# Context copies on ScalarE, router weights turned by TensorE, and additions in halves: one change to a two-layer attention kernel

## Chip, core and metric

The kernel runs on one core of a Trainium2 chip. The metric is the device time of one execution in microseconds (us); lower is better. The engines are TensorE (PE, its weight loads are PEld), VectorE (DVE), ScalarE (ACT), GpSimd (POOL) and SyncE (SP, which only issues DMAs here). Each runs its own list of instructions in the order in which it was written, and they meet through semaphores.

## What is computed

Two transformer layers with adaptive layer norm (six modulation rows from a condition vector), on 4 batches of 1024 tokens of width 128. Cut to what matters:

```python
# layer 0, attention: 16 heads of 64, causal
q, k, v = split(einsum('bse,ehd->bshd', x, w_qkv))
probs = softmax(where(mask, q @ k.T / sqrt(64), neg));  out = (probs @ v) @ w_out
# layer 0, second half: mixture of depths. 127 of the 1024 tokens are routed
weights = (x @ router_w)[..., 0] + router_b[0]
topv, topi = top_k(weights, 128);  sel = weights > topv[:, -1]
sel_idx = sort(topi[:, :127]);  x_sel = x[sel_idx]
hn = rmsnorm(x_sel, ln1)        # small attention (rope, masked), then
x2 = x1 + gelu(rmsnorm(x1, ln2) @ w1) @ w2      # x1 = x_sel + attention
out = scatter(x2 * weights[sel_idx]) + x * (1 - sel)
# layer 1: attention with 16 heads of 8 and a 3D rope, then 8 experts, best 2 of them
# a gate of layer 0 or 1 is sign(g) * max(|g|, 0.25), with sign(0) = 1
```

## The kernel before

**First attention (layer 0).** Heads go in pairs; there are 8 pairs for each batch, 32 in all (`n`, in batch `a = n // 8`). A pair has 12 items `m`: two halves `c` of 512 queries, and in each the key tiles `j` up to the diagonal. For an item TensorE makes transposed scores (`st_item`) in one pair of banks, ScalarE takes their exponentials (`exp_item`, L1524), TensorE multiplies them by the values (`pv_item`) and adds up in bank 4, and GpSimd adds the exponentials for the softmax sums (`add_up`, L816: `p_sum += ring`, 10 additions for each pair). The first tile of a half (`m` = 0 and `m` = 4) is written into `p_sum` itself, the others into a ring of three. Meanwhile the row maxima of pair `n + 1` are made: TensorE `max_item`, VectorE `row_max` (L1943). When a half is complete its contexts leave bank 4 for `oT` (`contexts`, L1964, VectorE, 128x512), and the first `pv_item` of the next half waits for that copy (semaphore `o_out`).

**Second attention (layer 1).** Its steps (`step1`) are others: VectorE takes maxima of 128x1024 (L2342), ScalarE exponentials of 128x512 (L1765). Twenty-three steps of its lead lie in the last pair of a first attention.

**The side chain.** All the rest (norms, modulation, routing, the routed tokens' attention and FFN, layer 1's projections, experts) is a serial chain of named steps, `MOD0`, `ADD1`, `MOD_ATTN`, `PREP`, `LNA`, `MOE`. `slots_of` spreads the chain of batch `a` over the 96 items of that batch's pairs, at equal distances; each engine does its part of a step at the end of its part of that item, ScalarE one item later. Names with `~` have no work on TensorE. The others use one bank (bank 5, `side`), in order: `side_free` makes TensorE wait until the step before has been read out (`side_out`). For the last batch the chain runs between the steps of the second attention (`late_steps_of`).

The places that matter here:

- `mod0` and `mod1` (L1539, L1545): TensorE makes modulation rows in `side`, ScalarE copies them out, VectorE's `gates` (L1926) makes five passes over two rows in SBUF (sizes 128x256).
- `w0`, `w1`, `~wcol`: the router weights come out as a row repeated on all partitions, `w_row`; VectorE needs them as columns `w_col`, one per tile of 128 tokens. It multiplies each tile by the identity and sums along the row (L2083, 8 instructions of 128x128), then copies to `extra` (L2085, L2086).
- `rmsnorm` (L2141 to L2144), in `pickT0` and `wo0`: a chain of 9 instructions for the inverse root on 128x1, in `rsqrt` (L1886): `scalar_tensor_tensor` and `tensor_tensor`, each waiting for the one before. The layer norms use the same `rsqrt` on 128x8.
- `row_max` of an item stands in VectorE's list behind whatever side step came before it, and TensorE's `max_item` waits until the maxima two uses earlier have left the bank.

What GpSimd does for an item, as it was:

```python
sv = p_sum[(2 * n + c) % 3][:, :, lo:]
pool.tensor_tensor(sv, sv, ring0[SLOT[m]][:, :, 0:HALF - lo], ALU.add).then_inc(sem("added"), 1)
```

## Time and profile before

| | us |
|---|---|
| median of 3 runs | 2725.14 (2724.52 to 2730.5) |
| the profiled execution | 2733.0 |
| its span, first to last instruction | 2731.2 |
| busy in it: TensorE | 2183.8 (80%) |
| VectorE | 1627.4 (60%) |
| ScalarE | 1276.4 (47%) |
| GpSimd | 804.2 (29%) |
| first attention's 8 pairs of batch 0 | 58 to 390 |
| batch 1, with side chain | 390 to about 745 |
| second attention of batch 0 | to 973 |
| first attention, batch 2 / batch 3 | 973 to 1384 / 1637 to 2047 |
| second attention, batch 1 / 2 / 3 | to 1637 / 2368 / 2652 |
| remaining chain of the last batch | 2652 to 2731 |

The engines work at the same time, so their busy times don't add up to the span. An engine's idle time matters only where another engine's wait follows from it. The profile names for each idle stretch what ended it. The granted clock is the share of TensorE's full 2.4 GHz; it stands at 1.0 or 0.5 at any moment, and a stretch shows the mean.

### The profile page before, as it was taken

What the parts mean: (1) busy time and instruction counts of PE and PEld (TensorE: products, weight loads), DVE (VectorE), ACT (ScalarE), POOL (GpSimd) and SP (SyncE); (2) the same over time, 40 slices, a digit from 0 to 9 for tenths busy, and PEclk for the clock granted to TensorE, in tenths of its full rate; (3) what the DMA queues carried; (4) which work ended last, traced back from release to release, by engine and by line L of the source; (5) the groups of instructions that cost most, each with busy time, mean ns of one, the idle gap of its engine ahead of it and who ended that gap; (6) DMA issues with size and microseconds to landing.
All of it is one profiled execution on the core that took longest, in us unless ns stands there. A gap on an engine that the chain in (4) does not pass through costs nothing.

```text
span 2731.2 us, 39653 instructions
## 1 busy us (share of the span) xinstructions
PE 2183.8 (80%) x14753; PEld 896.9 (33%) x14757; DVE 1627.4 (60%) x2829; ACT 1276.4 (47%) x2289; POOL 804.2 (29%) x618
## 2 busy tenths in 40 slices
PE   3989998899777887889868778888877677667876
PEld 2434443444321133444312123344432222121112
DVE  3454446556678556555676745655576776487732
ACT  1433333343358743343347763233336466537873
POOL 0665563443500033443411103443343000001203
PEclk9999998999899998989989998898998898869999
DMA  3000001001110010000210000000021100110000
GB/s 79 15 23 15 20 23 35 23 27 35 35 42 14 1 30 12 15 19 27 66 40 20 12 4 27 19 15 27 12 65 38 47 1 16 59 34 3 5 3 8
DMA packets 81199, 69.14 MB, mean 25 GB/s; under 512 B 46672, under 2 KB 62800, under 8 KB 80496
## 3 DMA queue, kind: packets, MB, share of 16 engines
q1 hardware_dynamic: 81008, 66.60, 9.0%
q8 instruction: 119, 1.95, 0.3%
q14 instruction: 72, 0.59, 0.1%
HBM read 57.58 MB, written 8.98 MB: 24 GB/s over the span
## 4 chain that ended last, share of the span: by engine, by line
PE 61%; DVE 22%; ACT 9%; issue 6%; SPq 2%; DMA 1%; POOL 0%; ACTq 0%; POOLq 0%; DVEq 0%
PE banks L875 59%; DVE pmax L2342 5%; ACT ring L1765 3%; DVE part_max L1943 2%; ACT p_sum L1765 1%; ACT room L1572 1%; SPq L666 1%; DVE ntmp L1892 1%; PE banks L1014 1%; DVE ntmp L1847 1%; DVE pick L2083 1%; DVE rstd L1894 1%; DVE h L1911 1%; DVE room L2092 1%; DVE stats L1899 1%
## 5 line engine op out<-in xcount | busy, mean ns | idle before, releaser
L816 POOL TENSOR_TENSOR p_sum<-p_sum,ring 128x1024 f32<-128x1024 f32 (+3 forms) x320 | 548.9, 1715 | 810.5 <-PE banks L875 453.0
L2342 DVE TENSOR_REDUCE pmax<-banks 128x2 f32<-128x1024 f32 x512 | 610.5, 1222 | 187.9 <-PE banks L875 184.6
L1943 DVE TENSOR_REDUCE part_max<-banks 128x2 f32<-128x1024 f32 (+3 forms) x384 | 365.8, 958 | 336.7 <-PE banks L875 334.2
L875 PE MATMUL banks<-ring,v 128*9 128x512 f32 (+4 forms) x2816 | 565.5, 581 | 0.0
L875 PE MATMUL banks<-qT,kT 64*128 64x512 f32 (+4 forms) x2048 | 468.3, 521 | 100.1 <-DVE pmax L2342 52.4
L1765 ACT ACTIVATE ring<-banks 128x512 f32<-128x512 f32 x768 | 416.3, 596 | 144.7 <-PE banks L875 141.5
L1524 ACT ACTIVATE ring<-banks 128x1024 f32<-128x1024 f32 (+3 forms) x320 | 245.7, 768 | 473.9 <-PE banks L875 468.6
L875 PE MATMUL banks<-oT 64*128 64x512 bf16 x1024 | 185.2, 397 | 91.6 <-ACT ring L1765 41.7
L875 PEld LDWEIGHTS banks<-qT,kT 64*128 64x128 f32 (+1 forms) x2048 | 147.7, 169 | 325.0 <-issue 101.5
L875 PE MATMUL banks<-p_sum,v 128*9 128x512 f32 (+1 forms) x768 | 220.4, 644 | 31.9 <-DVE oT L1964 26.3
L847 POOL TENSOR_TENSOR room<-room 128x512 f32<-128x512 f32 x32 | 40.6, 1270 | 691.5 <-ACT room L1572 691.5
L875 PE MATMUL banks<-k_bf,q_bf 64*128 64x512 bf16 (+3 forms) x768 | 133.8, 342 | 92.6 <-DVE part_max L1943 91.9
L1765 ACT ACTIVATE p_sum<-banks 128x512 f32<-128x512 f32 x256 | 139.0, 595 | 75.7 <-PE banks L875 75.7
L875 PEld LDWEIGHTS banks<-ring,v 128*9 128x9 f32 (+1 forms) x2816 | 95.2, 112 | 151.2 <-issue 76.4
L875 PE MATMUL banks<-kT,qT 64*128 64x512 bf16 x512 | 105.4, 408 | 45.5 <-ACT ring L1765 29.5
L875 PEld LDWEIGHTS banks<-oT 64*128 64x128 bf16 x1024 | 42.5, 94 | 299.4 <-ACT ring L1765 164.5
L794 POOL CAST q_bf<-qT 128x512 bf16<-128x512 f32 x64 | 39.3, 614 | 317.8 <-ACT qT L1482 317.7
L875 PE MATMUL banks<-hT,w_qk 128*128 128x512 f32 x256 | 129.9, 632 | 1.5 <-ACT hT L1529 0.9
L875 PE MATMUL banks<-m_row,ones_bf 64*128 64x512 bf16 (+3 forms) x768 | 130.7, 333 | 0.0
L1524 ACT ACTIVATE p_sum<-banks 128x1024 f32<-128x1024 f32 x64 | 65.5, 1023 | 123.3 <-PE banks L875 123.2
L1938 DVE COPY kT<-banks 128x512 f32<-128x512 f32 x64 | 43.3, 689 | 107.7 <-PE banks L875 107.1
L822 POOL TENSOR_TENSOR oT<-oT,inv_bc 128x1024 f32<-128x1024 f32 x32 | 76.3, 2385 | 90.9 <-DMA inv_bc<-softmax_inverses 90.9
(270 smaller groups left out, 2624.7 us busy)
## 6 DMA issues: line engine op xcount, KB each, us to landing
inv_bc<-softmax_inverses SPq DMA_DIRECT2D x64, 256.0 KB, 4.0
w_qk<-in_L_attn_w_qkv SPq DMA_DIRECT2D x64, 64.0 KB, 2.1
low<-in_L_ffn_attention_mask SPq DMA_DIRECT2D x4, 1024.0 KB, 6.1
stage<-rope_constants SPq DMA_DIRECT2D x4, 1024.0 KB, 4.8
x_b<-in_L_attn_x SPq DMA_DIRECT2D x4, 512.0 KB, 4.6
w_v<-in_L_attn_w_qkv SPq DMA_DIRECT2D x32, 64.0 KB, 2.1
stage<-in_L_ffn_w SPq DMA_DIRECT2D x8, 256.0 KB, 6.2
out<-x_b SPq DMA_DIRECT2D x16, 128.0 KB, 1.8
```

The source lines that it names most:

```text
L666: sp.dma_start(dst[rows, :, :], src[par, :, 2 * g:2 * g + 2, :]).then_inc(sem(f"stacks{g}"), 16)
L794: pool.tensor_copy(q_bf[:, cols], qT[q][:, cols]).then_inc(sem("qb_cast"), 1)
L816: pool.tensor_tensor(sv, sv, ring0[SLOT[m]][:, :, 0:HALF - lo], ALU.add).then_inc(sem("added"), 1)
L822: pool.tensor_tensor(ov, ov, inv_bc[:, :], ALU.mult).then_inc(sem("o_norm"), 1)
L847: pool.tensor_tensor(pv[:, 0:4, :], pv[:, 0:4, :], pv[:, 4:8, :], ALU.add).then_inc(sem("halved"), 1)
L875: return pe.matmul(dst, lhsT, rhs, start=start, stop=stop)
L1014: last = pe.transpose(side[:, (t % 4) * P:(t % 4 + 1) * P], src[:, t, :], eye)
L1524: act.activation(dst, banks[1][:, :, lo:HALF], ACT.Exp, scale=SCALE0).then_inc(sem("expd"), 1)
L1765: act.activation(ring1[n % 8], bank[ST1_BANK[n % 3]][:, :], ACT.Exp, scale=SCALE).then_inc(sem("expd1"), 1)
L1938: dve.tensor_copy(kT[n % 2][:, c * HALF:(c + 1) * HALF], bank[6 + c][:, :]).then_inc(sem("k_evac"), 1)
L1943: dve.reduce_max(part_max[:, :, t, c], banks[MAX_PAIR[m]][:, :, 0:w], AX).then_inc(sem("row_max"), 1)
L2342: dve.reduce_max(pmax1[:, :, g, t, c], banks[(0, 3)[USE1[b]["max", m] % 2]][:, :, :], AX).then_inc(sem("row_max1"), 1)
```

## The change

- `contexts` goes from VectorE's list to ScalarE's. There it stands behind the exponentials of the first item of the next half: half 0 of a pair behind `exp_item(n, 4)`, half 1 behind `exp_item(n + 1, 0)`. In the last pair of batches 1 to 3 half 1 stands behind its own last item.
- `add_up` makes two additions in place of one, one for each head of the pair, the second waiting for the first (new semaphore `added0`).
- `~wcol` becomes `wcol`, with work on TensorE: eight transposes of a 1x128 piece of `w_row` into one column each of `side`; VectorE copies the eight columns twice out of the bank. The row numbers in `extra` are written once, at setup.
- `mod0` and `mod1` have no copy on ScalarE; VectorE reads the bank itself, and `gates` has three instructions, of which the first two read the bank. The step `~gates0` is gone, and so the other steps of each chain lie up to one item earlier.
- `rmsnorm` uses a new `rsqrt_column`: nine `tensor_scalar` instructions whose second operand is a column of scalars. The layer norms keep `rsqrt`.

```diff
...
-MOD0 = ["mod0", "~gates0"]
+MOD0 = ["mod0"]
 ADD1 = ["mod1", "ctxT0", "ctxT1", "wo1_0", "wo1_1"]
...
        + [f"ex{n}" for n in range(2 * T)] + ["~moe"])
-MOD_ATTN = ["~lnb_a", "~lnb_b", "lnb0", "lnb1", "w0", "w1", "~wcol", "~larger0", "~larger1", "nb", "~sel", "thr", "slots", "~pick", "gather", "idx",
+MOD_ATTN = ["~lnb_a", "~lnb_b", "lnb0", "lnb1", "w0", "w1", "wcol", "~larger0", "~larger1", "nb", "~sel", "thr", "slots", "~pick", "gather", "idx",
             "pickT0", "pickT1", "maskrows", "hn1", "trig", "qkv", "rot0", "msel", "~kdiag", "sc0", "sc1", "pT0", "sc2", "pT1", "sc3", "pT2", "pT3",
...
                     sv = p_sum[(2 * n + c) % 3][:, :, lo:]
-                    pool.tensor_tensor(sv, sv, ring0[SLOT[m]][:, :, 0:HALF - lo], ALU.add).then_inc(sem("added"), 1)
+                    pool.tensor_tensor(sv[:, 0, :], sv[:, 0, :], ring0[SLOT[m]][:, 0, 0:HALF - lo], ALU.add).then_inc(sem("added0"), 1)
+                    pool.wait_ge(sem("added0"), NA * n + ADDED[m])
+                    pool.tensor_tensor(sv[:, 1, :], sv[:, 1, :], ring0[SLOT[m]][:, 1, 0:HALF - lo], ALU.add).then_inc(sem("added"), 1)
...
                 yield "mod0"
-                yield "~gates0"
...
                     yield f"w{c}"
-                for s in ("~wcol", "~larger0", "~larger1"):
-                    yield s
+                side_free(("wcol", b))
+                read_out(pe, ("w1", b))
+                for t in range(T):
+                    last = pe.transpose(side[:, t:t + 1], w_row[0:1, t * P:(t + 1) * P], eye[0:1, 0:1])
+                last.then_inc(sem("side_mm"), 1)
+                yield "wcol"
+                yield "~larger0"
+                yield "~larger1"
                 side_free(("nb", b))
...
             def mod0_side(b):
-                filled(act, ("mod0", b))
-                copy(mod0[b % 2][:, :, :].rearrange("p a d -> p (a d)"), side[:, :]).then_inc(sem("side_out"), 1)
                 yield "mod0"
-                yield "~gates0"
             def add1_side(m):
-                if m:
-                    act.wait_ge(sem("x_final"), T // 2 * m)
-                filled(act, ("mod1", m))
-                copy(mod1[:, :, :].rearrange("p a d -> p (a d)"), side[:, 0:2 * D]).then_inc(sem("side_out"), 1)
                 yield "mod1"
...
                     yield f"w{c}"
-                for s in MOD_ATTN[MOD_ATTN.index("~wcol"):MOD_ATTN.index("pickT0")]:
+                for s in MOD_ATTN[MOD_ATTN.index("wcol"):MOD_ATTN.index("pickT0")]:
                     yield s
...
+            def contexts(n, c):
+                act.wait_ge(sem("pv"), NI * n + (4 if c == 0 else NI))
+                if n >= OSLOTS:
+                    a, p = divmod(n - OSLOTS, NP)
+                    if p < OUT_PAIRS:
+                        filled(act, ("op0_1", a))
+                    elif a == 0:
+                        filled(act, ("op1_1", a))
+                    else:
+                        act.wait_ge(sem("out_mm"), 2 * a)
+                copy(oT[n % OSLOTS][:, c * HALF:(c + 1) * HALF], bank[4][:, :]).then_inc(sem("o_out"), 1)
...
                     exp_item(n, m)
+                    if m == 4:
+                        contexts(n, 0)
+                    if m == 0 and (p or a == 1):
+                        contexts(n - 1, 1)
+                    if m == NI - 1 and p == NP - 1 and a:
+                        contexts(n, 1)
                     if m == ROWS1_AT + 1:
...
             link(dve.tensor_scalar(an, an, 3.1415925, -3.1415925, ALU.min, ALU.max))
+            link(dve.tensor_copy(extra[:, :, 1], const("row")))
             dve.memset(extra[:, :, 0:1], 0.0).then_inc(sem("setup_dve"), 1)
...
                     link(dve.scalar_tensor_tensor(dst, t_, 1.5, cur, ALU.add, ALU.mult))
+                    cur = dst
+            def rsqrt_column(dst, src, bits, t_):
+                link(dve.tensor_scalar(bits, src.bitcast(I32), 1, None, ALU.logical_shift_right))
+                link(dve.tensor_scalar(bits, bits, -1.0, RSQRT_MAGIC, ALU.mult, ALU.add))
+                cur = bits.bitcast(F32)
+                for _ in range(3):
+                    link(dve.tensor_scalar(t_, cur, cur, -0.5, ALU.mult, ALU.mult))
+                    link(dve.tensor_scalar(t_, t_, src, 1.5, ALU.mult, ALU.add))
+                    link(dve.tensor_scalar(dst, t_, cur, None, ALU.mult))
                     cur = dst
...
-            def gates(mod, g):
+            def gates(dst, g):
                 ga = tmp[:, 0:2 * D].rearrange("p (a d) -> p a d", a=2)
-                link(dve.scalar_tensor_tensor(ga, g, -1.0, g, ALU.mult, ALU.max))
-                link(dve.tensor_scalar(ga, ga, 0.25, None, ALU.max))
-                link(dve.tensor_scalar(g, g, 0.0, 2.0, ALU.is_ge, ALU.mult))
-                link(dve.tensor_scalar(g, g, -1.0, None, ALU.add))
-                link(tt(g, g, ga, ALU.mult))
+                link(dve.tensor_scalar(dst, g, 0.0, 0.5, ALU.is_ge, ALU.subtract))
+                link(dve.scalar_tensor_tensor(ga, dst, 4.0, g, ALU.mult, ALU.mult))
+                return dve.scalar_tensor_tensor(dst, ga, 0.5, dst, ALU.max, ALU.mult)
...
-            def contexts(n, c):
-                dve.wait_ge(sem("pv"), NI * n + (4 if c == 0 else NI))
-                if n >= OSLOTS:
-                    a, p = divmod(n - OSLOTS, NP)
-                    if p < OUT_PAIRS:
-                        filled(dve, ("op0_1", a))
-                    elif a == 0:
-                        filled(dve, ("op1_1", a))
-                    else:
-                        dve.wait_ge(sem("out_mm"), 2 * a)
-                dve.tensor_copy(oT[n % OSLOTS][:, c * HALF:(c + 1) * HALF], bank[4][:, :]).then_inc(sem("o_out"), 1)
...
                 filled(dve, step)
-                dve.wait_ge(sem("gates0"), a + 1)
+                read_out(dve, ("mod0", a))
                 residual(xs3[a % 3], c, side[:, :], mod0[a % 2][:, 0, :]).then_inc(sem("side_out"), 1)
...
             def mod0_side(b):
+                m = mod0[b % 2]
+                filled(dve, ("mod0", b))
+                new = side[:, :].rearrange("p (a d) -> p a d", a=4)
+                link(dve.tensor_copy(m[:, 1, :], new[:, 1, :]))
+                link(dve.tensor_scalar(m[:, 2, :], new[:, 2, :], 1.0, None, ALU.add))
+                gates(m[:, 0::3, :], new[:, 0::3, :]).then_inc(sem("side_out"), 1)
+                read_out(dve, ("mod0", b))
                 yield "mod0"
-                read_out(dve, ("mod0", b))
-                m = mod0[b % 2]
-                gates(m, m[:, 0::3, :])
-                dve.tensor_scalar(m[:, 2, :], m[:, 2, :], 1.0, None, ALU.add).then_inc(sem("gates0"), 1)
-                yield "~gates0"
...
                 x = xs3[m % 3]
+                if m:
+                    dve.wait_ge(sem("x_final"), T // 2 * m)
+                filled(dve, ("mod1", m))
+                gates(mod1[:, :, :], side[:, 0:2 * D].rearrange("p (a d) -> p a d", a=2)).then_inc(sem("side_out"), 1)
+                read_out(dve, ("mod1", m))
                 yield "mod1"
-                read_out(dve, ("mod1", m))
-                gates(mod1, mod1[:, :, :])
                 yield "ctxT0"
...
                 filled(dve, ("lnb1", b))
-                dve.wait_ge(sem("gates0"), b + 1)
+                read_out(dve, ("mod0", b))
                 dve.wait_ge(sem("ln_b_h"), T * (b + 1))
...
                 yield "w1"
-                read_out(dve, ("w1", b))
-                for t in range(T):
-                    dve.scalar_tensor_tensor(ties[:, t, :], w_row[:, t * P:(t + 1) * P], 1.0, eye, ALU.mult, ALU.mult, accum_out=w_col[:, t:t + 1]).then_inc(sem("w_col"), 1)
-                dve.wait_ge(sem("w_col"), T * (b + 1))
-                link(dve.tensor_copy(extra[:, :, 0], w_col[:, :]))
-                link(dve.tensor_copy(extra[:, :, 1], const("row")))
-                yield "~wcol"
+                filled(dve, ("wcol", b))
+                link(dve.tensor_copy(extra[:, :, 0], side[:, 0:T]))
+                dve.tensor_copy(w_col[:, :], side[:, 0:T]).then_inc(sem("side_out"), 1)
+                read_out(dve, ("wcol", b))
+                yield "wcol"
                 if b:
...
                     link(dve.tensor_scalar(nvar[:, 0:1], nvar[:, 0:1], RMS_EPS, None, ALU.add))
-                    rsqrt(rstd[:, 0:1], nvar[:, 0:1], nbits[:, 0:1], ntmp[:, 0:1])
+                    rsqrt_column(rstd[:, 0:1], nvar[:, 0:1], nbits[:, 0:1], ntmp[:, 0:1])
                     dve.scalar_tensor_tensor(hn[:, :], src, rstd[:, 0:1], ln_rows[:, n, :], ALU.mult, ALU.mult).then_inc(sem("hn"), 1)
...
                                 final_max(n + 1, 0)
-                    if m == 4:
-                        contexts(n, 0)
                     if m == 5 and (p or a == 1):
                         invert(n - 1)
-                    if m == NI - 1:
-                        contexts(n, 1)
                     for step in SLOT_STEPS[a][p * NI + m]:
...
```

ScalarE's list in the second pair of batch 0, from `m` = 2 to `m` = 6, as it was (`p_sum` and `ring` are the exponentials, `m_row`, `qT` and `v` the next pair's row maxima, queries and values):

```order
L1524 ACTIVATE ring<-banks 128x2x128
L1482 ACTIVATE m_row<-banks 128x512
L1482 ACTIVATE qT<-banks 128x512 x2
L1524 ACTIVATE p_sum<-banks 128x1024
L1524 ACTIVATE ring<-banks 128x1024
L1482 ACTIVATE v<-banks 128x512 x2
```

and as it is now:

```order
L1531 ACTIVATE ring<-banks 128x2x128
L1489 ACTIVATE m_row<-banks 128x512
L1489 ACTIVATE qT<-banks 128x512 x2
L1531 ACTIVATE p_sum<-banks 128x1024
L1489 ACTIVATE oT<-banks 128x512
L1531 ACTIVATE ring<-banks 128x1024
L1489 ACTIVATE v<-banks 128x512 x2
```

The context copy stands between the exponentials of items 4 and 5. It stands in the same way behind the `p_sum` of item 0.

VectorE's list in batch 2's side chain, where the router weights become columns, as it was (`part_max` and `max_cols` are the row maxima of the next pair, `cnt` counts larger weights):

```order
L1938 COPY kT<-banks 128x512 x2
L1964 COPY oT<-banks 128x512
L1847 TENSOR_TENSOR h<-h,mod 128x8x128
L1943 TENSOR_REDUCE part_max<-banks 128x2 x2
L1970 RECIPROCAL inv_pk<-den_pk 128x16
L2083 SCALAR_TENSOR_TENSOR pick,w_col<-w_row,consts 128x128 x8
L2085 COPY h<-w_col 128x8
L2086 COPY h<-consts 128x8
L1943 TENSOR_REDUCE part_max<-banks 128x2
L2092 TENSOR_SCALAR room,cnt<-w_row,w_col 128x1024
```

and as it is now:

```order
L1967 COPY kT<-banks 128x512 x2
L2103 COPY h<-banks 128x8
L2104 COPY w_col<-banks 128x8
L1972 TENSOR_REDUCE part_max<-banks 128x2 x2
L1986 RECIPROCAL inv_pk<-den_pk 128x16
L2111 TENSOR_SCALAR room,cnt<-w_row,w_col 128x1024
```

The `oT` copy is gone from here, eight multiplications and two copies have become two copies, and the step stands one item earlier, ahead of the two maxima of item 5; the counting (`~larger0`) follows those maxima directly.

## Rows read from the trace of the kernel before

**Rows 1.** Stretches from:to in us, length, each engine's busy us; PEclk is the granted clock.

```profile
core 0: us, PE busy (x) PEld busy (x) DVE busy (x) ACT busy (x) POOL busy (x), PEclk, DMA share, GB/s
58.00:390.00 332.00, 310.37 (x2284) 138.94 (x2282) 154.95 (x216) 126.84 (x173) 188.75 (x132) 0.97 0.08 20
322.90:356.80 33.90, 32.94 (x254) 14.36 (x248) 14.63 (x19) 13.81 (x20) 21.61 (x16) 1.00 0.10 23
390.00:706.00 316.00, 277.02 (x1890) 140.58 (x1890) 190.41 (x395) 109.98 (x182) 131.82 (x91) 0.92 0.10 28
600.60:651.40 50.80, 48.09 (x348) 26.27 (x345) 31.36 (x70) 17.09 (x24) 21.66 (x15) 1.00 0.11 36
1009.00:1328.00 319.00, 270.28 (x1808) 134.33 (x1808) 187.68 (x350) 106.41 (x177) 127.02 (x88) 0.89 0.08 22
1671.00:1987.00 316.00, 268.07 (x1804) 133.06 (x1801) 187.17 (x350) 106.77 (x179) 126.69 (x88) 0.89 0.07 18
```

**Rows 2.** TensorE's waits, 58 to 390 us: total us, times, longest.

```profile
PE banks L875 <- DVE part_max L1943: 14.1, 11, 7.9
```

**Rows 3.** TensorE's waits, 390 to 706 us.

```profile
PE banks L875 <- DVE part_max L1943: 12.4, 7, 5.3
PE banks L875 <- DVE oT L1964: 10.6, 6, 2.8
...
PE banks L1176 <- DVE hn L2144: 3.5, 1, 3.5
```

**Rows 4.** TensorE's waits, 1009 to 1328 us.

```profile
PE banks L875 <- DVE part_max L1943: 30.4, 11, 6.9
...
PE banks L875 <- DVE oT L1964: 4.0, 4, 3.4
```

**Rows 5.** Timeline around `~wcol` of batch 2: start, us, instruction, [idle before it].

```profile
1051.55 2.36 POOL L816 TENSOR_TENSOR p_sum<-p_sum,ring 128x1024 f32<-128x1024 f32 x1 [0.28 <-ACT ring L1524]
...
1051.56 2.49 DVE L2083 SCALAR_TENSOR_TENSOR pick<-w_row,consts 128x128 f32<-128x128 f32 x1
...
1062.43 0.61 PE L875 MATMUL banks<-k_bf,q_bf 64*128 64x512 bf16 x2 [6.89 <-DVE part_max L1943]
```

**Rows 6.** Timeline at the second `rmsnorm` of batch 2's chain.

```profile
1210.26 2.35 DVE L1892 SCALAR_TENSOR_TENSOR ntmp<-nbits 128x1 f32<-128x1 f32 x1
...
1219.48 0.29 PE L875 MATMUL banks<-k_bf,q_bf 64*128 64x128 bf16 x2 [6.70 <-DVE part_max L1943]
```

**Rows 7.** Groups by line and shape, whole span: busy us, mean ns of one | idle before.

```profile
L816 POOL TENSOR_TENSOR p_sum<-p_sum,ring 128x1024 f32<-128x1024 f32 x128 | 301.1, 2352 | 319.2 <-PE banks L875 201.2 <-ACT ring L1524 118.0
...
L816 POOL TENSOR_TENSOR p_sum<-p_sum,ring 128x512 f32<-128x512 f32 x64 | 82.8, 1294 | 92.5 <-ACT ring L1524 89.6
...
L1014 PE MATMUL banks<-consts,h 128*128 128x128 f32 x128 | 27.6, 354 | 62.4 <-DVE h L1911 59.9 <-ACT den_rows L1482 1.5 <-ACT hT L1529 0.9
...
L849 POOL TENSOR_TENSOR room<-room 128x256 f32<-128x256 f32 x32 | 23.3, 728 | 2.5
...
L1892 DVE SCALAR_TENSOR_TENSOR ntmp<-rstd 128x1 f32<-128x1 f32 x16 | 11.4, 714 | 0.6
```

**Rows 8.** One line's instructions: ns min/median/max of one, first and last start.

```profile
L2142 DVE TENSOR_SCALAR nvar<-nvar x8: 153/154/154, 491.1 to 2291.5; 128x1 f32<-128x1 f32 x8
```

**Rows 9.** The same for the multiplications of `~wcol`.

```profile
L2083 DVE SCALAR_TENSOR_TENSOR pick<-w_row,consts x32: 279/289/2494, 436.1 to 2162.9; 128x128 f32<-128x128 f32 x32
```

**Rows 10.** Timeline where half 0's contexts leave bank 4, a pair of batch 0.

```profile
144.09 1.02 ACT L1524 ACTIVATE p_sum<-banks 128x1024 f32<-128x1024 f32 x1 [0.68 <-PE banks L875]
...
146.99 0.68 DVE L1964 COPY oT<-banks 128x512 f32<-128x512 f32 x1
...
147.81 1.08 PE L875 MATMUL banks<-p_sum,v 128*64 128x512 f32 x4 [0.20 <-DVE oT L1964]
```

**Rows 11.** Timeline: a pair's last two additions, and item 1's exponential of the next.

```profile
131.33 2.13 POOL L816 TENSOR_TENSOR p_sum<-p_sum,ring 128x512 f32<-128x512 f32 x2
...
135.23 0.81 ACT L1524 ACTIVATE ring<-banks 128x768 f32<-128x768 f32 x1 [1.28 <-PE banks L875]
```

More of the change, by code:

```diff
@@ L490, in adaln_kernel @@
                  den_stored den_loaded inv_den inv_stored inv_loaded o_norm out_mm res_a
-                 ln_a_h ln_b_h ln_c_h ln_d_h gates0 w_col larger thr_part sel trig_rep pick mask_pick hn rot_s k_diag mask_sel sc_max sc_exp proc
+                 ln_a_h ln_b_h ln_c_h ln_d_h larger thr_part sel trig_rep pick mask_pick hn rot_s k_diag mask_sel sc_max sc_exp proc
                  split_h split_m split_l rope1 rest1
                  s1_mm row_max1 nmax_hl mrow1_mm mrow1 st1_mm expd1 pv1 o1_raw ctx_raw ctx1
-                 lg_sub lg_exp coef halved moe gated x_final
+                 lg_sub lg_exp coef added0 halved moe gated x_final
         """.split() + [f"scratch_{a}{part}" for a in "qk" for part in "hml"] + [f"stacks{g}" for g in range(NG)] + [f"x_in{n}" for n in range(3)]
```

## The prediction

> **What bounds the kernel now.** I read the busy times by stretch first, because a share over the whole span mixes two kinds of stage. In the first attention of batch 0 TensorE is the bound: an undisturbed pair takes 33.90 us and TensorE is busy for 32.94 of them, at clock 1.00 [rows 1]. In the same attention of batches 1, 2 and 3 the side chain runs along. A pair can still go at full clock there (50.80 us with 48.09 busy, in the stretch where the chain has the most matmul work), but over the eight-pair stretches TensorE is idle for 39, 49 and 48 us, and the granted clock is 0.92, 0.89 and 0.89 [rows 1]. The last two batches have the same numbers within 3 us, so I work out batch 2 and count it twice.
>
> Next come the waits: who makes TensorE idle? Nearly always VectorE, and under two names. The row maxima (`part_max`) cost 14.1, 12.4 and 30.4 us in batches 0, 1 and 2, and the context copy (`oT`) 10.6 and 4.0 us in batches 1 and 2 [rows 2 to 4]. Neither is slow itself. Both stand in VectorE's list behind a side step. So the third view is the timeline just before a wait. At 1062.43 TensorE goes on after 6.89 us of idling for a maximum. Before that VectorE was in the multiplications of `~wcol`, one of which took 2.49 us, starting and ending with a GpSimd addition of 2.36 us [rows 5]. The same instruction has a minimum of 279 ns and a median of 289 [rows 9]. In `rmsnorm` an operation on 128x1 takes 2.35 us, and TensorE's wait at the end of that chain is 6.70 us [rows 6]; its mean over 16 is 714 ns [rows 7]. But the `tensor_scalar` on 128x1 in the same chain never took more than 154 ns, all eight of them [rows 8]. So some of VectorE's instructions wait until the running GpSimd addition is over, and others never do. That is what four of the change's five edits touch.
>
> **Edit 1, contexts on ScalarE.** VectorE loses 64 copies of 0.68 us, ScalarE gets 64. In an undisturbed pair TensorE waited 0.20 us for the copy [rows 10]. On ScalarE it starts when the exponential ends, 144.09 + 1.02 = 145.11, and even at VectorE's 0.68 us it is over by 145.8, two microseconds before TensorE's 147.81. So the wait goes: 8 x 0.2 = 1.6 us in batch 0. ScalarE is busy for a third to two fifths of these stretches, and what stands behind the copy on it, the next exponential, waits for TensorE. I take nothing as its cost. In batches 1 to 3 the waits of 10.6, 4.0 and again 4.0 us go, 18.6. In the last pair of these batches the copies lie among maxima of the second attention, with VectorE the engine that ends the waits; two copies of 0.68 in each of three give 4 us. Together **24 us**.
>
> **Edit 2, `wcol` on TensorE.** VectorE's part falls from eight multiplications and two copies to two small copies out of a bank. The longest waits, 5.3 in batch 1 and 6.9 in batch 2, lie on it [rows 3, 4]; I take them as gone: 5.3 + 6.9 + 6.9 = **19 us**. It adds eight transposes to TensorE. The trace has none of 1x128. The nearest are those of 128x128, 27.6 us for 128 [rows 7], or 0.22 each, so 1.7 us for eight at the most; the least is nothing. I take 1 us, four times: -4. In batch 3's chain, which lies in the second attention, no addition runs: there eight times 0.289 us become two copies, **2 us** at most.
>
> **Edit 3, `rmsnorm` on columns.** It has nine instructions as before. If a `tensor_scalar` with a column of scalars behaves like the one with a constant [rows 8], none waits for GpSimd. Batches 1 to 3 have two each. Waits that go with them: 3.5 in batch 1 and, of the other maxima waits there (12.4 - 5.3 = 7.1 in six), about 4; in batch 2 6.7 and one that I put at 5 of the remaining 30.4 - 6.9 - 6.7; batch 3 as batch 2. That is 7.5 + 11.7 + 11.7 = 31, less 1 us for each of the six that stays, since the first and last instruction of a `rmsnorm` still read two arrays of 128x128: **25 us**.
>
> **Edit 4, additions in halves.** GpSimd's additions take 2352 ns for 1024 columns and 1294 for 512, that is 236 ns fixed; the step from one to the next dependent one is 2.5/32 = 0.08 us [rows 7]. An addition becomes 0.31 us longer, and 320 of them 100 us. Is GpSimd's list on the path? The nearest place is the ring: a pair's last addition ends at 131.33 + 2.13 = 133.46, and the exponential that may need its slot starts at 135.23, 1.8 us later [rows 11]. Half 1 has seven additions, 2.2 us more in all, part of which goes into the idle time ahead of them (0.28 us ahead of the one in [rows 5]). So it just fits, at nothing. The gain: a VectorE instruction waits for the rest of 1.29 us, not of 2.35. On the layer norms' `rsqrt`, which is not changed, it takes perhaps 5 of batch 0's 14.1 us [rows 2], and 2 us in each other batch: **11 us**.
>
> The Trainium skill, "SBUF — State Buffer", section "Who interferes with whom", has this as an exclusive lock on a port pair that VectorE and GpSimd share, held for the whole instruction; by that rule the trace agrees (2.49 us beside 2.36). The same page counts `tensor_scalar` among those that can take the pair. By that, edit 3 would bring nothing, and the sum below would be 25 us smaller plus its share of clock; the 154 ns of a 128x1 speak against it.
>
> **Edit 5, gates from the bank.** Of five or six instructions on SBUF arrays two now remain that read no bank. In batches 2 and 3 the `mod0` step lies on a maxima wait; I take 2 us each: **4 us**. VectorE now waits for TensorE's matmul in the very item of the step, behind which the next maxima are queued: at `mod0` and `wcol`, some 0.5 us six times, -3. In the last chain, where nothing covers it, `ctxT0` comes after three VectorE operations and no longer after one copy: -1.
>
> **The clock.** Where the clock is low TensorE's work takes twice its time. The loss is the missing share times the busy time: 0.08 x 277 = 22, 0.11 x 270 = 30 and again 30, 82 us in all [rows 1]. The granted clock is 1.00 in the pairs with little idling and 0.89 to 0.92 where there is much [rows 1]. As some two thirds of the waits on VectorE go, but not all and not the ones for norms, I take half: **41 us**. Bounds are 0 and 82.
>
> **Sum:** 24 + 19 + 2 + 25 + 11 + 4 + 41 = 126, less 4 + 3 + 1 = 8, gives 118 us. The profiled execution has a span of 2731.2 us and took 2733.0; the runs' median is 2725.1. Off the span that gives 2613; off the median **2607 us**.
>
> **Rivals.**
>
> A. The waits pass to the next thing. All steps come up to an item earlier, and a side step of 2 us, ahead of a maximum, makes TensorE wait even with no GpSimd in play. Then half of the 83 us of waits goes and the clock gives back a tenth of its 82: 42 + 8 + 2 - 8 = 44 us, 2681 us. For it: eleven maxima waits in batch 2, with only three explained above. Against: those three are 20 of 30 us. Chance 0.2, anywhere from 2650 to 2690.
>
> B. The columns wait all the same. Edit 3's 25 us and some 10 of clock are missing: 2642 us. For it: a column of scalars is a form the trace does not have at 128x1. Chance 0.07. (The Trainium skill's line on `tensor_scalar` in the same section of "SBUF — State Buffer" would have it so.)
>
> C. GpSimd becomes the bound, and the kernel slower. The gain is 118/32 = 3.7 us for a pair. With the 1.8 us of slack, additions of half 1 may become (3.7 + 1.8)/7 = 0.79 us longer each before it is used up; 0.31 is what I count. A VectorE instruction slipping in between two halves can add its own time. At 1.0 us the change would cost 7.0 - 1.8 - 3.7 = 1.5 us a pair, 48 in all: 2773 us. Chance 0.04.
>
> D. ScalarE holds things up: its copy waits for `pv_item`, the exponentials behind it come late, and TensorE with them, by 0.6 us at each of 64. The gain falls by 38 us: 2645 us. ScalarE's idle stretches speak against it. Chance 0.05.
>
> **How the numbers follow.** The forecast has 0.64, from 2570 (the clock all but restored) to 2650. The range of 8 in 10 takes in B and D and most of A: 2570 to 2675. A measurement of this kernel tells 0.2%, some 5 us, from no change. Slower by over that: C, 0.04. Within: 0.02, between A and C. Faster: 0.94.
>
> **What would show it.** In the profile after: no long waits for `oT` (now ScalarE's) and none behind `wcol`; `rsqrt_column`'s instructions at 154 to 170 ns without exception; VectorE instructions of the layer norms at 1.3 us at most when they wait; additions at 1.29 us with gaps of 0.08; mean clock in the stretches of batches 1 to 3 about 0.95; undisturbed pairs of batch 0 at 33.7 us. An exponential that waits for `p_sum` additions by more than a few microseconds in all would show C, a copy out of bank 4 ahead of an idle TensorE D.

## The result, and the profile after

| | before | after |
|---|---|---|
| median of 4 runs, us | 2727.06 (2724.52 to 2730.5) | 2625.34 (2620.49 to 2626.73) |
| ratio | | 0.9623, 95% interval 0.9605 to 0.9641 |
| span of the profiled execution | 2731.2 | 2623.9 |
| busy: TensorE / VectorE | 2183.8 / 1627.4 | 2150.5 / 1524.6 |
| busy: ScalarE / GpSimd | 1276.4 / 804.2 | 1305.8 / 872.7 |

The change takes off 102 us; from span to span it is 107.3, since the traced execution of before (2733.0 us) is slower than the four of its runs. Of the 107.3 TensorE is busy 33.3 us less, with no matmul left out, and the other 74.0 are idle time that is gone.

For the stretches I cut at the first exponential of a batch's first pair and of its second attention. (The stretch 58:390 of [rows 1] also holds most of batch 1's first pair; the right cut for batch 0 is 65.0 to 359.4.) The windows of before, for batches 0 to 3, columns as in [rows 1]:

```profile
65.00:359.40 294.40, 275.74 (x2043) 124.38 (x2045) 138.34 (x195) 112.13 (x154) 170.30 (x119) 0.98 0.08 19
359.40:758.50 399.10, 346.90 (x2395) 167.88 (x2390) 241.34 (x453) 138.01 (x220) 173.15 (x117) 0.93 0.10 29
975.10:1383.50 408.40, 344.26 (x2332) 165.73 (x2332) 247.50 (x422) 137.12 (x219) 170.28 (x115) 0.91 0.10 28
1639.60:2046.50 406.90, 343.13 (x2334) 165.77 (x2332) 247.56 (x422) 137.13 (x219) 170.36 (x115) 0.91 0.10 27
```

and of after, with the undisturbed pair of batch 0 as first line:

```profile
323.60:357.50 33.90, 32.97 (x252) 14.33 (x250) 13.43 (x18) 14.80 (x21) 23.44 (x26) 1.00 0.09 23
...
66.10:357.50 291.40, 277.08 (x2044) 124.55 (x2046) 121.05 (x179) 118.88 (x168) 184.13 (x197) 0.97 0.08 20
357.50:735.10 377.60, 340.06 (x2402) 164.63 (x2398) 222.32 (x419) 146.40 (x235) 191.99 (x199) 0.95 0.10 30
947.40:1312.50 365.10, 330.20 (x2340) 156.79 (x2340) 215.18 (x387) 144.52 (x234) 188.32 (x195) 0.96 0.11 31
1566.20:1936.00 369.80, 333.27 (x2340) 158.49 (x2340) 215.37 (x387) 144.58 (x233) 188.45 (x195) 0.95 0.10 30
```

The first attentions give 3.0, 21.5, 43.3 and 37.1 us. The rest of the span gives 2.4 us in all. In batch 2 TensorE's idle time falls from 64.1 to 34.9 us, its busy time by 14.1 with the clock from 0.91 to 0.96. The undisturbed pair has not become shorter: 33.90 us, as in [rows 1].

TensorE's waits in that batch (947.4 to 1312.5; total us, times, longest), beside [rows 4]:

```profile
PE banks L877 <- DVE part_max L1972: 10.9, 11, 5.2
PE banks L877 <- DVE pmax L2361: 9.1, 7, 3.5
...
PE banks L1016 <- DVE h L1942: 1.9, 1, 1.9
```

The 30.4 us of waiting for maxima are 10.9, and no wait for `oT` is left. On ScalarE the copy stands where the order shows it (timeline of a pair in batch 0, beside [rows 10]):

```profile
146.95 1.02 ACT L1531 ACTIVATE p_sum<-banks 128x1024 f32<-128x1024 f32 x1 [0.68 <-PE banks L877]
147.87 0.59 ACT L1489 ACTIVATE oT<-banks 128x512 f32<-128x512 f32 x1
...
150.40 1.08 PE L877 MATMUL banks<-p_sum,v 128*64 128x512 f32 x4
```

It ends at 148.46, 1.9 us before TensorE's `p_sum` multiplication, which now starts with no idle time ahead of it. `wcol` on TensorE is eight transposes in 0.65 us:

```profile
1013.48 0.65 PE L1075 MATMUL banks<-consts,w_row 1*128 1x1 f32 x8
```

The instructions of `rmsnorm` and of the counting, by line (ns min/median/max of one, first and last start):

```profile
L1923 DVE TENSOR_SCALAR ntmp<-rstd x16: 211/214/216, 476.5 to 2184.1; 128x1 f32<-128x1 f32 x16
...
L1924 DVE TENSOR_SCALAR ntmp<-ntmp,nvar x24: 212/214/215, 476.0 to 2184.3; 128x1 f32<-128x1 f32 x24
...
L1925 DVE TENSOR_SCALAR rstd<-ntmp,rstd x16: 211/214/215, 477.0 to 2184.6; 128x1 f32<-128x1 f32 x16
...
L2111 DVE TENSOR_SCALAR_CACHE_REDUCE room<-w_row,w_col x32: 340/805/1269, 435.2 to 2059.1; 128x1024 bf16<-128x1024 f32 x4, 128x896 bf16<-128x896 f32 x4, 128x768 bf16<-128x768 f32 x4, 128x640 bf16<-128x640 f32 x4
...
L1942 DVE TENSOR_SCALAR h<-x_b,mv,rstd x128: 333/341/1161, 38.9 to 2566.0; 128x128 f32<-128x128 f32 x128
```

There are 72 column instructions (L1923 and L1925 have eight more each, which read `nbits`). None of them ever waited: 216 ns at most, though 42 of the 72 start while a `tensor_tensor` of GpSimd's is running. The longest wait that is left in batch 2 is a new one, at the next side step that reads two arrays in SBUF (`~larger1`, L2116, the ties):

```profile
1026.87 2.36 POOL L824 TENSOR_TENSOR oT<-oT,inv_bc 128x1024 f32<-128x1024 f32 x1
1027.16 2.21 DVE L2116 SCALAR_TENSOR_TENSOR pick<-w_row,w_col,consts 128x128 f32<-128x128 f32 x1
1029.18 0.77 POOL L816 TENSOR_TENSOR p_sum<-p_sum,ring 128x256 f32<-128x256 f32 x1
...
1034.73 0.40 PE L877 MATMUL banks<-k_bf,q_bf 64*128 64x256 bf16 x2 [5.18 <-DVE part_max L1972]
```

It meets the normalisation (L824), which the change leaves whole: that adds 1.9 us to the first of this step's eight instructions, usually 0.34 us each, and the halved additions behind it add 1.4 us to four others. The longest wait of all for a maximum is now one of 6.3 us in batch 0, at 174 us, behind a layer norm.

### The profile page after: what moved, and what is told of

Read it like the earlier page. It is cut to its first block, busy times and chain, and to the rows that moved or that the text cites. A ratio compares the mean times of both kernels' runs of the same rounds, so it can differ in the third digit from the quotient of the medians.

```text
span 2623.9 us, 39960 instructions
## 1 busy us (share of the span) xinstructions
PE 2150.5 (82%) x14785; PEld 878.7 (33%) x14789; DVE 1524.6 (58%) x2690; ACT 1305.8 (50%) x2345; POOL 872.7 (33%) x938
## 4 chain that ended last, share of the span: by engine, by line
PE 63%; DVE 19%; ACT 9%; issue 6%; SPq 3%; DMA 1%; POOL 0%; ACTq 0%; POOLq 0%; DVEq 0%
PE banks L877 61%; DVE pmax L2361 5%; ACT ring L1778 3%; DVE part_max L1972 3%; ACT p_sum L1778 2%; ACT room L1572 2%; SPq L666 1%; PE banks L1016 1%; DVE room L2111 1%; DVE stats L1930 1%; DVE tmp L1866 1%; DVE room L1866 1%; DVE h L1942 1%; ACT oT L1489 1%; PE banks L1366 1%
## 5 line engine op out<-in xcount | busy, mean ns | idle before, releaser
L877 PE MATMUL banks<-ring,v 128*9 128x512 f32 (+4 forms) x2816 | 553.6, 573 | 0.0
L816 POOL TENSOR_TENSOR p_sum<-p_sum,ring 128x512 f32<-128x512 f32 (+3 forms) x320 | 306.3, 957 | 613.9 <-ACT ring L1531 338.4
L818 POOL TENSOR_TENSOR p_sum<-p_sum,ring 128x512 f32<-128x512 f32 (+3 forms) x320 | 309.6, 967 | 25.1
L877 PE MATMUL banks<-p_sum,v 128*9 128x512 f32 (+1 forms) x768 | 214.8, 629 | 2.1 <-ACT p_sum L1778 2.1
```

The lines of the kernel that those rows point to most:

```text
L816: pool.tensor_tensor(sv[:, 0, :], sv[:, 0, :], ring0[SLOT[m]][:, 0, 0:HALF - lo], ALU.add).then_inc(sem("added0"), 1)
L818: pool.tensor_tensor(sv[:, 1, :], sv[:, 1, :], ring0[SLOT[m]][:, 1, 0:HALF - lo], ALU.add).then_inc(sem("added"), 1)
L877: return pe.matmul(dst, lhsT, rhs, start=start, stop=stop)
```

## Experiments

Twelve kernels. First, one edit undone in the changed kernel, four times. The theory was that the forecast's terms add up: undoing one gives back its term and its share of the clock. The rival: some terms are empty, or stand in for each other.

**Contexts back on VectorE.**

```diff
-                copy(oT[n % OSLOTS][:, c * HALF:(c + 1) * HALF], bank[4][:, :]).then_inc(sem("o_out"), 1)
+                dve.tensor_copy(oT[n % OSLOTS][:, c * HALF:(c + 1) * HALF], bank[4][:, :]).then_inc(sem("o_out"), 1)
```

> The changed kernel with one edit undone: VectorE copies the contexts again (edit 1). By the sum's terms: 24 us of waits and a third of the clock's 41, some 35 us, scaled to the 102 us measured for all: about 30 us over the changed kernel, 2655 us, and TensorE's waits for the oT copy are back, 10 us in batch 1. By rival A (waits pass on to the next thing) the copies count for less, since other side steps delay the maxima beside them: within 8 us of the changed kernel, 2625 to 2633 us.

Measured: 2648.89 us, ratio to before 0.9713 (0.9694 to 0.9732), so 23.6 us lost. That lies between the 30 us of the forecast's terms and rival A's 8. TensorE's waits over its whole span have the copy again:

```profile
PE banks L877 <- DVE oT L1973: 19.7, 25, 3.4
```

**Router weights turned on VectorE**, with the eight multiplications and the name `~wcol`, at the new items.

```diff
-                    last = pe.transpose(side[:, t:t + 1], w_row[0:1, t * P:(t + 1) * P], eye[0:1, 0:1])
+                    dve.scalar_tensor_tensor(ties[:, t, :], w_row[:, t * P:(t + 1) * P], 1.0, eye, ALU.mult, ALU.mult, accum_out=w_col[:, t:t + 1])
```

> The changed kernel with VectorE's eight multiplications for the router columns again (edit 2). By the terms: 19 us of waits, less 4 for the transposes and 1.5 for VectorE's wait, and 9 of clock: about 20 us over the changed kernel, 2645 us. By the rival that with halved additions these multiplications wait only half as long anyway: 10 us over, 2635 us; each should then take 1.3 us at most.

Measured: 2625.37 us, ratio 0.9625 (0.9605 to 0.9645). Nothing is lost. My expectation fell.

**The old `rsqrt` in `rmsnorm`.**

```diff
-                    rsqrt_column(rstd[:, 0:1], nvar[:, 0:1], nbits[:, 0:1], ntmp[:, 0:1])
+                    rsqrt(rstd[:, 0:1], nvar[:, 0:1], nbits[:, 0:1], ntmp[:, 0:1])
```

> The changed kernel with the old chain of scalar_tensor_tensor and tensor_tensor in rmsnorm (edit 3). By the terms: 25 us and 12 of clock, scaled: about 32 us over, 2657 us. Rival: halved additions have already taken half of each of these waits (2.3 us become 1.3), so the column form is worth about 15 us, 2640 us.

Measured: 2630.62 us, ratio 0.9653 (0.9632 to 0.9675): 5.3 us lost, where the forecast's term is 25 and even the rival expected 15.

**Whole additions.**

```diff
-                    pool.tensor_tensor(sv[:, 0, :], sv[:, 0, :], ring0[SLOT[m]][:, 0, 0:HALF - lo], ALU.add).then_inc(sem("added0"), 1)
-                    pool.wait_ge(sem("added0"), NA * n + ADDED[m])
-                    pool.tensor_tensor(sv[:, 1, :], sv[:, 1, :], ring0[SLOT[m]][:, 1, 0:HALF - lo], ALU.add).then_inc(sem("added"), 1)
+                    pool.tensor_tensor(sv, sv, ring0[SLOT[m]][:, :, 0:HALF - lo], ALU.add).then_inc(sem("added"), 1)
```

> The changed kernel with whole additions on GpSimd again (edit 4). By the terms 11 us and 5 of clock are lost: about 14 us over, 2639 us; VectorE's waiting instructions take up to 2.35 us. Rival: with edits 2 and 3 in place few instructions are left that wait, and GpSimd's 100 us more are on the path: within 5 us of the changed kernel or under it, 2615 to 2630 us.

Measured: 2621.55 us, ratio 0.9615 (0.959 to 0.964), 3.8 us less than the changed kernel and inside what these runs can tell apart.

Undone one by one the edits are worth 23.6 + 0 + 5.3 + 0, some 29 of 102 us. So either they stand in for each other, or something else carries the rest: the items, which move with the dropped `~gates0`, or the gates. The next four kernels ask that.

**All three undone together** (router weights, `rsqrt`, halves: the three diffs above), at the new items.

> The changed kernel with three edits undone together: the router weights turned by VectorE, the old rsqrt in rmsnorm, and whole additions; contexts stay on ScalarE, the gates stay read from the bank. One by one these three cost nothing, 5 and nothing when undone. If that is all they are worth, the time is 2625 + 5 = 2630 us (2620 to 2638). If each stands in for the others (a wait on a GpSimd addition is avoided twice or thrice over, so that one missing edit does no harm), their value shows only here: 30 to 55 us with the clock, 2655 to 2680 us, with the long waits behind the multiplications (5 to 7 us) and behind rmsnorm (7 us) back.

Measured: 2640.76 us, ratio 0.9685 (0.967 to 0.9699). That is 15.4 us for the three against 5.3 one by one. They do stand in for each other, but it is not the 30 to 55 us I looked for.

**Only the contexts moved**, on the kernel before (the first diff the other way round).

> The kernel before with only the contexts on ScalarE. Undone alone in the changed kernel this edit was worth 24 us. If it is worth the same here, 2703 us (2698 to 2708). The forecast's terms, 24 of waits and a third of the clock's 41, give 2727 - 38 = 2689. If it is the edit that carries the whole, since it takes VectorE's list out of TensorE's way whatever the others do, 2650 or less.

Measured: 2680.47 us, ratio 0.9827 (0.9811 to 0.9844): 47 us alone, twice what undoing it costs, and between the expectations of 2689 and 2650. TensorE's 26.3 us of waits for `oT` over the whole span are gone, and in the four first attentions it is busy 18.4 us less.

**The changed kernel at the old items**, with an empty step on each engine:

```diff
-MOD0 = ["mod0"]
+MOD0 = ["mod0", "~gates0"]
...
+                yield "~gates0"
```

> The changed kernel with an empty step where ~gates0 was, so that the side chain's steps lie at their old items; everything else as changed. If the items don't matter: 2625 us within 4. If a good part of the gain comes from the steps lying up to an item earlier (the same work beside other exponentials and additions, ahead of other maxima), it is lost here: 2640 to 2660 us.

Measured: 2623.25 us, ratio 0.9622 (0.9605 to 0.964). Nothing is lost.

**Edit 5 undone whole**, with the copies on ScalarE, the five passes and the old items.

```diff
-                gates(m[:, 0::3, :], new[:, 0::3, :]).then_inc(sem("side_out"), 1)
+                gates(m, m[:, 0::3, :])
...
+                yield "~gates0"
```

> The changed kernel with edit 5 undone: ScalarE copies mod0 and mod1 out, VectorE makes five passes in SBUF, the step ~gates0 is back and with it the old items. The forecast's terms for it are +4, -3 and -1, so 2625 us within 4. If the items or the five passes on SBUF arrays carry more than counted, 2640 to 2660 us; the difference from the run with the empty step alone is then what the passes themselves cost.

Measured: 2625.05 us, ratio 0.9621 (0.9604 to 0.9638). Nothing either.

From the contexts alone (2680.5) to the contexts with edit 5 (2640.8) there are 40 us, but with the three other edits in place edit 5 is worth nothing. Either its passes or its shift of the items does what the three others do too.

**Contexts and gates, at the old items**: the kernel at 2640.8 us with the empty step.

> Contexts on ScalarE and the gates read from the bank, everything else as before, and the steps at their old items (an empty step stands where ~gates0 was). With the steps at their new items this kernel took 2640.8 us, and with the contexts alone 2680.5. If the new items made that difference (in the run at 2640.8 the eight multiplications of the router weights met no addition, 0.29 us each, where they took up to 2.4 us before), this one takes 2665 to 2678 us, and only the wait behind the gates (3.4 us in each of batches 2 and 3, with its clock) is gone. If the passes read from the bank made it, 2640 to 2648 us.

Measured: 2672.43 us, ratio 0.98 (0.9783 to 0.9816). The passes are worth 8 us, the shift of the items 32. The traces show how. At the old items the multiplications of batch 2 meet one whole addition after the other:

```profile
1027.84 2.49 POOL L816 TENSOR_TENSOR p_sum<-p_sum,ring 128x1024 f32<-128x1024 f32 x1 [0.28 <-ACT ring L1524]
...
1028.06 2.43 DVE L2099 SCALAR_TENSOR_TENSOR pick<-w_row,consts 128x128 f32<-128x128 f32 x1
...
1030.50 4.42 POOL L816 TENSOR_TENSOR p_sum<-p_sum,ring 128x1024 f32<-128x1024 f32 x2 [0.17 <-ACT ring L1524]
...
1030.63 2.43 DVE L2099 SCALAR_TENSOR_TENSOR pick<-w_row,consts 128x128 f32<-128x128 f32 x1
...
1038.65 0.61 PE L875 MATMUL banks<-k_bf,q_bf 64*128 64x512 bf16 x2 [6.83 <-DVE part_max L1966]
```

At the new items (the kernel at 2640.8 us) the same eight instructions fall into a gap of GpSimd's:

```profile
1013.35 0.29 DVE L2096 SCALAR_TENSOR_TENSOR pick<-w_row,consts 128x128 f32<-128x128 f32 x1 [0.89 <-ACT w_row L1579]
...
1014.85 0.28 DVE L2096 SCALAR_TENSOR_TENSOR pick<-w_row,consts 128x128 f32<-128x128 f32 x1
...
1015.04 2.35 POOL L816 TENSOR_TENSOR p_sum<-p_sum,ring 128x1024 f32<-128x1024 f32 x1 [5.48 <-ACT ring L1523]
```

GpSimd had been idle for 5.48 us, and the last multiplication starts 0.19 us before it goes on. Over all 32 of them the mean is 469 ns there and 832 ns at the old items. TensorE's wait of 5.87 us behind the first `rmsnorm` of batch 2 is gone too; the one behind the second stays (6.70 and 6.88 us). Batch 3 is as batch 2. In batch 1 it goes the other way: the wait behind the multiplications is 5.35 us at the old items and 7.09 at the new. So the shift changes what each step meets, and here the sum of it is a gain.

This goes far to explain why undoing edit 2 in the changed kernel costs nothing: in batches 2 and 3 the multiplications meet no addition there. In batch 1 they do (TensorE waits 6.39 us behind them, and 2.69 in the changed kernel), and that stretch is 3.3 us longer. In the trace batch 3's stretch is 5.3 us shorter, which hides it; why is not shown.

**Whole additions at the old items**, edits 1, 2, 3 and 5 in place.

> The changed kernel with two parts undone: the additions whole, and the empty step back, so that the items are the old ones. Undone alone, neither cost anything. If halves are worth what the waits of 2.35 us cost at the old items, 2640 us. If halves pay for themselves no more than they cost (the undisturbed pair is 33.9 us with halves and 33.6 without, 0.3 x 32 = 10 us), the same 2622 us within 5, or 2612 at best.

Measured: 2625.16 us, ratio 0.9622 (0.9604 to 0.964). The halves bring nothing at these items either, once edits 2 and 3 are in.

**Halves alone at the old items**, on the kernel at 2672.4 us.

> The kernel at 2672.4 us (contexts on ScalarE, gates from the bank, steps at their old items, everything else as before) with the additions in halves and nothing more. There the multiplications of the router weights and rmsnorm still meet additions, which edits 2 and 3 no longer do. If halves are worth the forecast's 11 us where the other two edits are absent, 2661 us. If they cut every wait to nearly half, they get half of the 47 us that edits 2 and 3 bring at these items, 2649 us, and so stand in for them. If they are worth nothing anywhere (a second half makes the next instruction wait again, and a pair is 0.3 us longer), 2672 to 2682 us.

Measured: 2643.79 us, ratio 0.969 (0.9669 to 0.9711): 28.6 us, more even than the 23 of the second expectation. The same stretch of multiplications there (VectorE's timeline):

```profile
1029.36 1.35 DVE L2101 SCALAR_TENSOR_TENSOR pick<-w_row,consts 128x128 f32<-128x128 f32 x1
...
1030.97 1.11 DVE L2103 COPY h<-w_col 128x8 f32<-128x8 f32 x1
```

So the longest of them wait 1.1 us each where it was 2.1, and TensorE's wait behind them falls from 6.83 to 1.98 us.

Seven of the kernels make a table. All have the contexts on ScalarE and the gates from the bank; medians in us:

| | neither | halves | edits 2 and 3 | halves, 2 and 3 |
|---|---|---|---|---|
| old items | 2672.4 | 2643.8 | 2625.2 | 2623.3 |
| new items | 2640.8 | not run | 2621.6 | 2625.3 |

Where nothing else is done each of the three means brings 29 to 47 us; where edits 2 and 3 are in, the other two bring nothing that can be measured.

**The additions cut to one column**, on the kernel before; the softmax sums are left out.

```diff
-                    pool.tensor_tensor(sv, sv, ring0[SLOT[m]][:, :, 0:HALF - lo], ALU.add).then_inc(sem("added"), 1)
+                    pool.tensor_tensor(sv[:, 0, 0:1], sv[:, 0, 0:1], ring0[SLOT[m]][:, 0, 0:1], ALU.add).then_inc(sem("added"), 1)
```

> The kernel before, but GpSimd adds one column where it added up to 1024, so the softmax sums of the first attention are left out; nothing else is changed. It puts a bound on all that edits 2 to 4 can gain. If the long instructions of VectorE (116 us over their usual length in the kernel before) come from GpSimd's additions and TensorE waits for them, the waits behind the multiplications, rmsnorm and the norms go and some of the clock comes back: 2640 to 2670 us. If TensorE's waits are mostly VectorE's list as such, and the long instructions only fill time that is there: 2700 us or more.

Measured: 2616.38 us, ratio 0.9585 (0.9561 to 0.9608), 110 us under before and so more than I had put as the most. TensorE's wait for maxima in batch 2 is

```profile
PE banks L875 <- DVE part_max L1943: 11.7, 12, 3.0
```

against 31.5 in the same batch of the kernel before (from 30.4 in [rows 4], which leave out its ends). What VectorE's instructions take over the median of their line and shape is 115 us before, 17 here and 64 in the changed kernel. Here GpSimd's additions are shown to be the cause, not only neighbours in the timeline, and they cost 110 us with all the edits undone. The run takes away every way from an addition to TensorE, not only the one over VectorE. The others were small before: ScalarE's exponentials waited for additions twice, 4.7 us in all, and an undisturbed pair takes 33.80 us here for 33.90.

## Why the prediction was right, and which of its terms were not

The time of 2607 us came out as 2625.3, inside the range. The sum was 118 us; the medians give 102 and the two traces 107.3.

**The frame held.** TensorE waits for VectorE because VectorE waits for GpSimd's additions: the run with small additions shows it. The terms without the clock were 77 us; TensorE's idle time fell by 74.0. The clock's term was 41, half of what the low clock cost; TensorE's busy time fell by 33.3, two fifths. That half was chosen between the bounds 0 and 82 and not worked out, so its coming near is in part luck. The clocks of batches 1 to 3, 0.95 to 0.96, are as forecast.

**Edit 1, contexts: 24.** The mechanism is as told: the waits for `oT` are gone, ScalarE's copy is over 1.9 us early, and undoing it costs 23.6 us. But the term is without the clock. Alone on the kernel before it brings 47: in batch 2 16.0 us, of which TensorE's idle time is 8.3 and its busy time, at clock 0.93 for 0.91, is 7.7. The term's size was right for idle time alone. Batch 0 gave 1.8 for the 1.6 counted (an undisturbed pair goes from 33.90 to 33.60).

**Edit 2, `wcol`: 19, less 4.** The waits of 5.3 and 6.9 us were there and are gone. The step that failed is to credit them to this edit alone: the shift by one item, which I had as a fact of the change and priced only as a danger (rival A), removes those of batches 2 and 3 too, though not that of batch 1. The transposes cost 0.65 us each time, a third less than I took. My 2 us in batch 3's late chain didn't come: the last stretch, from batch 2's second attention on, is 3 us longer (687.9 for 684.7). In it TensorE now waits three times for ScalarE's copy `oT` (4.1 us) and stands idle twice for 1.8 us with nothing named, which the kernel before doesn't have, nor the one with the router weights turned on VectorE (its stretch takes 685.2). That points at the `wcol` step. But the kernels with that step have anything from 682.8 to 690.3 us there, so it isn't shown.

**Edit 3, `rmsnorm`: 25.** That columns never wait is right, which decides against rival B. Their 154 to 170 ns are wrong: 214, so nine instructions are 0.4 us longer where nothing collides. Undone in the changed kernel the edit is worth 5.3 us. The likely reason is that the halves have already cut its waits: at the same items with whole additions edits 2 and 3 are worth 19.2 us together (2640.8 to 2621.6), with halves 0 and 5.3 one by one. Edit 3 alone was not tried with whole additions. It was mis-sized as a share, not as a sum: edits 2 and 3 together bring 47 us at the old items with whole additions, and the terms 19 - 4 + 25 with a third of the clock make some 53.

**Edit 4, halves: 11, at no cost.** Both halves of this are off. The cost: the last two pairs of batch 0, undisturbed, take 33.6 to 33.7 us in every kernel with contexts on ScalarE and whole additions, 33.9 to 34.0 with halves, so the gain of the contexts there is used up, 0.3 us a pair. TensorE's waits of the changed kernel from 190 to 400 us show it, in a kind that no kernel with whole additions has in that stretch:

```profile
PE banks L877 <- issue: 1.0, 6, 0.2
```

No releaser is named, but all six stand before the same matmul, the first that multiplies the next pair's keys `k_bf`. It needs GpSimd's cast of the keys (the program waits there for the semaphore `kb_cast`), and in GpSimd's list that cast stands behind an addition. In the changed kernel:

```profile
339.46 1.26 POOL L816 TENSOR_TENSOR p_sum<-p_sum,ring 128x512 f32<-128x512 f32 x1 [4.62 <-ACT ring L1531]
...
340.80 1.26 POOL L818 TENSOR_TENSOR p_sum<-p_sum,ring 128x512 f32<-128x512 f32 x1
...
342.00 1.17 POOL L804 CAST k_bf<-kT 128x512 bf16<-128x512 f32 x2
...
342.71 0.23 PE L877 MATMUL banks<-k_bf,q_bf 64*128 64x128 bf16 x2 [0.16 <-issue]
```

and with whole additions (the kernel at 2640.8 us):

```profile
332.41 2.35 POOL L816 TENSOR_TENSOR p_sum<-p_sum,ring 128x1024 f32<-128x1024 f32 x1 [4.62 <-ACT ring L1523]
...
334.71 1.17 POOL L804 CAST k_bf<-kT 128x512 bf16<-128x512 f32 x2
...
335.42 0.23 PE L875 MATMUL banks<-k_bf,q_bf 64*128 64x128 bf16 x2
```

One cast takes 0.61 us, so TensorE starts 0.10 us behind the end of the first in both. From the addition's start to the matmul it is 3.25 us with halves and 3.01 without, which is nearly all of the 0.3. So the step that failed is where I looked for GpSimd's slack: at the ring, where there is some (ScalarE's `ring` exponentials wait 1.7 us in all, three times, for the second halves), and not at its other work in the same list, where there is none. Rival C's mechanism is real there, but costs 0.3 us a pair and not 1.5. This is read from the traces; no run moves the cast. The gain: 28.6 us where nothing else is done, none where edits 2 and 3 are. By the runs the changed kernel would be as fast without this edit. The sign that layer norm instructions would wait 1.3 us at most failed too: one took 2.33, beside the normalisation, which is not halved.

**Edit 5, gates: 4, less 3 and 1.** The passes are worth 8 us beside the contexts alone, nothing in the changed kernel. (Of the three instructions of the new `gates` one reads no bank, not two.) The shift of the items, which the prediction had only in rival A and as a loss, is a gain of 32 us where the other edits are missing, and nothing where they are in.

**Rival A** came in part: a wait of 5.18 us stands at the ties (L2116). But it takes the place of 6.89, and the three long waits did not return elsewhere in full. **Rival D** has nothing for it: no wait of TensorE's in a first attention ends with ScalarE's copy `oT`. Over the whole span four do (4.9 us), all in second attentions.

**What was missed.** The sum came out near because I counted each wait once, by its place in the trace. The names on the terms were arbitrary: many a wait had two or three removers.

The Trainium skill, "SBUF — State Buffer", section "Who interferes with whom", leaves out `tensor_scalar` with an accumulator and counts the plain one among those that can take the shared pair, when its operands meet certain conditions. The trace agrees for L2111, with an accumulator, which never waited, and for L1942, plain and 128x128, which did (341 ns at the median, 1161 at most). Plain 128x1 never did, in 72 instructions with a column. The prediction took the rule without those conditions, and by that edit 3 would have brought nothing; the measurement decides.

## What to carry to other kernels

When two engines collide, count each wait once and don't sum the edits: an edit's worth is the wait that no other edit removes. To know which edits to keep, undo them in groups and not only one by one; here one by one found 29 of 102 us. A side step that reads SBUF twice can be cured by moving it by one item into a gap of the other engine, but such a place is kept by chance, and the same shift made a wait longer in another batch: edits 2 and 3, which take the collision itself away, made the time the same at both placements (2625.2 and 2621.6 us). And before an engine off the path is given longer work, look for its slack at everything that stands in its list: the ring had 1.8 us, the cast in the same list none.

## What the runs showed of the hardware

- A `tensor_scalar` of 128x1 with a column as second operand takes 214 ns (211 to 216, 72 instructions), the one with constants in the same chain 154. The `scalar_tensor_tensor` that it replaces takes 160 where it doesn't wait.
- Neither form of `tensor_scalar` waited for GpSimd at 128x1 in these traces. At 128x8 with constants it does: in the changed kernel one of a line that usually takes 0.17 us took 2.33 and another 0.95.

```profile
166.44 2.33 DVE L1937 TENSOR_SCALAR nvar<-mv 128x8 f32<-128x8 f32 x1
```

- Whether it is the number of columns that decides, and why, is open.
- An addition of one column on GpSimd takes 215 ns, so nearly all of the 236 ns that I had as the fixed part from two sizes. By form, in the kernel with small additions:

```profile
L816 POOL TENSOR_TENSOR p_sum<-p_sum,ring 128x1 f32<-128x1 f32 x320 | 68.9, 215 | 1161.3 <-ACT ring L1524 679.3 <-PE banks L875 482.0
```

- Two dependent additions of 128x512 take 2.60 us on GpSimd, from the start of the first to the end of the second (339.46 to 342.06), where one of 128x1024 takes 2.35.
